# A graph layer on one core: one stage in TensorE's loop, single buffers, and paced gathers in the opening

## The chip, the core and the metric

The kernel runs on one core of a Trainium2 chip. The metric is the time of one launch on the device, in microseconds (us). The engines are named as the profile names them: PE is TensorE (PEld its weight loads), DVE is VectorE, ACT is ScalarE, POOL is GpSimd, SP is SyncE, which only issues DMAs here.

## What is computed

Inputs: 12,500 nodes with 16 channels (`x`), 400,000 edges with a source and a destination node (`src`, `dst`, sorted by `dst`), and two tables of edge attributes with 16 and 2 columns.

```python
dx = maximum(edge_attr_2[:, 0], 1e-6); inv_dx = 1 / dx
slope_e = edge_attr_2[:, 1] * inv_dx
diff = (x[dst] - x[src]) * inv_dx[:, None]
d1 = segment_sum(diff, dst) - segment_sum(diff, src)
S  = segment_sum(slope_e, dst)
u  = x - clip(dt, 0.01, 2.0) * (x * d1 + g * S)
x  = layernorm(x + u)
sums, counts = segment_sum(edge_attr_16, dst), segment_sum(ones, dst)
x  = layernorm(x + sums / where(counts > 0, counts, 1))
```

So each edge needs two rows of `x`, one by its destination and one by its source, and its payload is added at both ends.

## The kernel before

**Tiling.** The edges are cut into C = 125 chunks of 3,200; a chunk is 25 tiles (`J`) of 128 edges, one edge per partition. Since `dst` is sorted, the destinations of a chunk lie in a window of 112 nodes. The sources lie anywhere.

**The steps of a chunk**, in the order in which they depend on each other:

1. ACT `node_hot` (L506, L508) turns the chunk's destinations (`rel_all`, broadcast to all partitions by SP's `load_rel`) into the one-hot matrix `node_of_dst`.
2. PE `take_row` (L572), 25 narrow matmuls, takes x[dst] out of the window `xwin` (SP's `load_window`) into `ps_x`. The last of them raises `x_dst_ready`.
3. DVE piece `x_of_dst` (L792) reads it, `x_in` tells PE by `x_dst_added`; `diff` (L843) subtracts x[src], which 25 indirect gathers on POOL (L412) have brought; then `pay`, `lo`, `scale`, `scaled`, `left`, `parts` on DVE with casts on ACT between them (L480 or L489, L482, L484, L486).
4. DVE `dst_hot` (L924, five instructions) makes the one-hot matrix of the destinations, and PE `take_sum` (L583), 25 narrow matmuls, adds the chunk up into its window; DVE piece `window` (L893) adds that to `dst_sum`.
5. DVE `spread` (L882, ten instructions: five groups of five tiles, called fives here, in two halves k each) lays the payload out by the low three bits of the source.
6. The main work: for each tile DVE makes a one-hot row block of the source's high bits (`one_hot`, L947, 128x1568, one slot of the ring `hi_hot`), and PE multiplies it with the tile's two halves of `spread`: 2 x 4 matmuls of 128x392 (`tile`, L630 the first of four, L635 the other three), added up in `ps_src` over all 3,125 tiles.

**Staging.** Stage c does the main work of chunk c, steps 3 to 5 of chunk c+1 between the tiles of DVE (`PIECES` says after which tile), the sums of chunk c+1 on PE in its tiles 11 to 19, and the rows of chunk c+2 on PE in its tiles 0 to 12. PE's and DVE's loops hold two stages (`Fori(0, PAIRS)`), and `xwin`, `node_of_dst`, `dst_of_node` and `spread` have two buffers, by parity of the chunk.

**What sets the order.** Each engine runs its list in order, and semaphores join them. `hi_hot_free` starts at the credit `RING` (10) and is raised by PE with the last matmul of every tile; DVE asks for it at every fifth tile (`HOTS_FREE`), so at tile 5 of a chunk it needs all 25 tiles of the chunk before to be done. PE waits for `hi_hot_ready` every second tile. POOL's gathers come in groups of five, each waiting for `hi_hot_free` as well, but the 75 gathers of chunks 0, 1 and 2 wait for nothing but their indices. A chunk's spreads are announced once, by `chunk_ready`.

**The opening.** Before PE's loop stand `x_of_dst(0)`, `window_sums(0)` and `x_of_dst(1)`, each a run of 25 narrow matmuls. Tile 0 of stage 0 waits for the whole of chunk 0's spreads and, because the rows of chunk 2 begin with it, for `x_dst_added` of chunk 1 and `node_hot` of chunk 2.

## Time and profile before

| | |
|---|---|
| median of 3 runs | 5045.37 us (5037.35 to 5047.1) |
| the profiled execution | 5042.16 us |
| its span | 5040.3 us |
| PE busy | 4590.3 us, 91% of the span |
| DVE busy | 3983.5 us, 79% |
| POOL busy | 3415.4 us, 68% |
| ACT busy | 1446.6 us, 29% |
| granted clock of PE over the span | 0.975 |
| PE's first main matmul starts at | 112.81 us |

The profiled execution is 1.9 us longer than its span (5042.16 - 5040.3) and 3.2 us under the median. A row of a timeline gives the start, the busy time, the instructions that were joined, and in brackets how long the engine had stood idle and what ended it: `<-issue` is time in which it waited for nothing that the profile shows, `<-remote` is a semaphore whose raiser was done long before.

### The profile page before, as it was taken

What the parts mean: (1) busy time and instruction counts of PE and PEld (TensorE: products, weight loads), DVE (VectorE), ACT (ScalarE), POOL (GpSimd) and SP (SyncE); (2) the same over time, 40 slices, a digit from 0 to 9 for tenths busy, and PEclk for the clock granted to TensorE, in tenths of its full rate; (3) what the DMA queues carried; (4) which work ended last, traced back from release to release, by engine and by line L of the source; (5) the groups of instructions that cost most, each with busy time, mean ns of one, the idle gap of its engine ahead of it and who ended that gap; (6) DMA issues with size and microseconds to landing.
All of it is one profiled execution on the core that took longest, in us unless ns stands there. A gap on an engine that the chain in (4) does not pass through costs nothing. (4 is left out here: it accounts for less than half of the span.)

```text
span 5040.3 us, 72091 instructions
## 1 busy us (share of the span) xinstructions
PE 4590.3 (91%) x31379; PEld 1240.2 (25%) x12630; DVE 3983.5 (79%) x8600; ACT 1446.6 (29%) x1018; POOL 3415.4 (68%) x3133
## 2 busy tenths in 40 slices
PE   1999999999999999999999899999999999999997
PEld 0222222222222222222222222222222222222222
DVE  4887778778877787778887787778787788787887
ACT  3322232222322232222322233222322233222320
POOL 5667667767677677676677667767676776776760
PEclk8999999999999999999999999999999999999998
DMA  3111111111111111111111111111111111111110
GB/s 75 31 36 35 31 31 31 40 31 31 31 32 39 31 31 31 39 31 31 31 31 39 31 31 31 32 39 31 31 31 38 33 31 31 31 39 31 31 29 7
DMA packets 210295, 167.87 MB, mean 33 GB/s; under 512 B 124650, under 2 KB 193774, under 8 KB 210024
## 3 DMA queue, kind: packets, MB, share of 16 engines
q1 hardware_dynamic: 109798, 139.79, 8.7%
q0 software_dynamic: 100000, 25.80, 6.6%
q10 hardware_dynamic: 476, 2.01, 0.1%
q8 instruction: 11, 0.18, 0.0%
q14 instruction: 10, 0.08, 0.0%
HBM read 164.55 MB, written 2.81 MB: 33 GB/s over the span
## 5 line engine op out<-in xcount | busy, mean ns | idle before, releaser
L412 POOL DMA_INDIRECT x_src<-in_x_dram,src_i x3125 | 3410.5, 1091 | 1492.9 <-issue 871.0
L635 PE MATMUL ps_src<-hi_hot,spread_lo 128*128 128x392 bf16 x18750 | 4210.7, 332 | 77.7 <-issue 75.9
L947 DVE TENSOR_SCALAR hi_hot<-col_h,hi_f,scale 128x1568 bf16<-128x1568 f16 x3125 | 2238.7, 723 | 482.0 <-remote 270.3
L630 PE MATMUL ps_src<-hi_hot,spread_lo 128*128 128x392 bf16 x6250 | 2075.6, 332 | 210.0 <-issue 140.4
L630 PEld LDWEIGHTS ps_src<-hi_hot,spread_lo 128*128 128x128 f16 x6250 | 620.7, 99 | 1319.2 <-issue 952.8
L882 DVE TENSOR_TENSOR spread_lo<-spread_lo,halves 128x640 f16<-128x640 f16 x1250 | 616.8, 494 | 60.1 <-issue 59.9
L583 PEld LDWEIGHTS ps_w<-dst_of_node,parts 128*102 128x102 bf16 x3125 | 392.3, 126 | 1050.9 <-issue 1011.6
L572 PEld LDWEIGHTS ps_x<-xwin,node_of_dst 112*128 112x128 bf16 x3125 | 305.8, 99 | 1358.3 <-issue 1348.7
L572 PE MATMUL ps_x<-xwin,node_of_dst 112*128 112x48 bf16 x3125 | 584.5, 190 | 49.2 <-issue 41.7
L583 PE MATMUL ps_w<-dst_of_node,parts 128*102 128x112 bf16 x3125 | 501.3, 213 | 51.4 <-DVE parts L871 41.5
L482 ACT CAST parts<-pay 128x425 bf16<-128x425 f32 x125 | 72.4, 579 | 1616.0 <-DVE pay L846 1500.7
L496 ACT CAST parts<-a 128x400 bf16<-128x400 f32 x125 | 71.4, 571 | 1258.5 <-DVEq L909 765.0
L508 ACT ACTIVATE node_of_dst<-node_of_dst,ones 128x3200 bf16<-128x3200 bf16 x125 | 370.3, 2962 | 4.1
L506 ACT ACTIVATE node_of_dst<-rel_all,row_neg 128x3200 bf16<-128x3200 f16 x125 | 369.8, 2959 | 2.6 <-DMA rel_all<-rel_d 2.6
L489 ACT COPY spread_lo<-lo_hot 128x3200 f16<-128x3200 f16 x124 | 352.8, 2845 | 0.0
L792 DVE TENSOR_REDUCE x_dst<-ps_x 128x160 f32<-128x480 f32 x375 | 192.1, 568 | 193.4 <-issue 141.5
L924 DVE TENSOR_TENSOR dst_of_node<-col_h,dst_rel 128x560 bf16<-128x560 f16 x625 | 276.1, 443 | 1.0 <-issue 1.0
L484 ACT CAST halves<-scaled 128x400 f16<-128x400 f32 x125 | 65.6, 525 | 401.4 <-DVE scaled L860 310.7
L893 DVE TENSOR_TENSOR dst_sum<-dst_sum,ps_w 102x112 f32 x125 | 33.8, 271 | 163.6 <-remote 92.5
L940 DVE TENSOR_TENSOR left<-a,parts 128x400 f32<-128x400 f32 x125 | 72.1, 577 | 85.9 <-ACT parts L496 45.6
L486 ACT CAST parts<-left 128x425 bf16<-128x425 f32 x125 | 72.4, 579 | 87.3 <-issue 48.2
L498 ACT CAST parts<-left 128x400 bf16<-128x400 f32 x125 | 71.7, 574 | 80.4 <-DVE left L940 48.9
(114 smaller groups left out, 1200.5 us busy)
## 6 DMA issues: line engine op xcount, KB each, us to landing
rel_all<-rel_d SPq DMA_DIRECT2D x125, 800.0 KB
x_src<-in_x_dram,src_i POOLq DMA_INDIRECT x3125
a<-in_edge_attr_dram SPq DMA_DIRECT2D x125, 200.0 KB
a<-in_edge_attr_dram SPq DMA_DIRECT2D x125, 25.0 KB
src_i<-in_src_dram SPq DMA_DIRECT2D x125, 12.5 KB
dst_i<-in_dst_dram SPq DMA_DIRECT2D x125, 12.5 KB
xwin<-xparts_d SPq DMA_DIRECT2D x125, 10.5 KB
dst_sum<-in_dst_dram SPq DMA_DIRECT2D x1, 1400.0 KB
```

The costliest lines, as they stand in the source:

```text
L412: nc.gpsimd.indirect_dma_start(x_src[:, b, j * F:(j + 1) * F], None, x[:, :], bass.IndirectOffsetOnAxis(ap=src_i[:, b, j:j + 1], axis=0)). ...
L489: nc.scalar.copy(lo_rows[:, :, :, :], bc(lo_hot[:, :, :], 3, F)).then_inc(lo_rows_ready, 1)
L506: nc.scalar.activation(node_of_dst[:, b, :, :], rel_all[:, :, :], ACT.Abs, bias=row_neg[:, 0:1], scale=1.0).then_inc(node_diff_ready, 1)
L508: nc.scalar.activation(node_of_dst[:, b, :, :], node_of_dst[:, b, :, :], ACT.Relu, bias=ones[:, 0:1], scale=-1.0).then_inc(node_hot_ready, 1)
L572: return nc.tensor.matmul(ps_x[:, j // PER, (j % PER) * SPL * F:(j % PER + 1) * SPL * F], nodes[0:WIN, j, :], window, start=True, stop=True)
L583: return nc.tensor.matmul(ps_w[0:SPL * V, 0:WIN], parts[:, j, :, :].rearrange("p k v -> p (k v)"), hots[:, j, :], start=(j == 0), stop=(j ...
L630: return nc.tensor.matmul(out_bank, weights, moving, start=False, stop=stop)
L635: return nc.tensor.add_instruction(mybir.InstMatmult(name=nc.get_next_instruction_name(), engine=pe.engine, start_tensor_calc=False, stop_ ...
L792: yield v.tensor_reduce(out_t[:, q * PER:q * PER + n, :], ps_x[:, q, 0:n * SPL * F].rearrange("p (j k f) -> p j f k", k=SPL, f=F), AX, ALU ...
L882: ins = v.tensor_tensor(spread[:, b, five, q, :, :], lo_rows[:, five, :, :], bc(halves[:, five, q, :], 2, LO), ALU.mult)
L924: ins = v.tensor_tensor(dst_of_node[:, b, five, :].rearrange("p j (n t) -> p j n t", t=2), bc(col_h[:, 0:WIN].rearrange("p (n t) -> p n t" ...
L947: v.tensor_scalar(hi_hot[:, slot(b, j), :], col_h[:, :], hi_f[:, b, j:j + 1], scale[:, b, j:j + 1], ALU.is_equal, ALU.mult).then_inc(hi_ho ...
```

## The change

**PE's loop** holds one stage, run C-2 times. Its body reads the same addresses in every round: `xwin`, `node_of_dst`, `dst_of_node` and `spread` have one buffer each, the ring's slot is the tile's number modulo 13 and no longer depends on the chunk's parity, and the credit is `LEAD` = 12. DVE's, ACT's, SP's and POOL's loops still hold two stages.

**Spreads.** With one buffer, a five can be written only when PE has done the same five of the chunk before. `spread_half` waits for that and raises `spread_ready` per five; PE waits for it at tiles 0, 5, 10, 15 and 20. Six of a chunk's ten halves are made in the stage before, four (`late`) at tiles 2, 3, 8 and 8 of its own.

**The other single buffers.** `dst_hot` is made one chunk ahead, not two, at the same tiles of the stage; `dst_rel` and its copy `rel2` are two pieces. `node_hot(m)` waits for `x_dst_ready` of m (before m-1). SP loads the next window when `x_dst_ready` comes, and `rel_all` after `node_diff_ready`, no longer after `attr_left`.

**The opening.** Of chunk 1's gathers the first five are free, and its four other groups wait for `pay_ready`, `parts_ready` and the first `spread_ready` of chunk 0, and for its first tile; the groups of chunk 2 wait for every fourth tile. `x_of_dst(1)` stands ahead of `window_sums(0)` on PE; on ACT, `node_hot(1)` waits for `x_dst_ready` of chunk 0 and stands ahead of `finish(0)`, `node_hot(2)` ahead of `begin(1)`.

```diff
-    RING = 10
+    RING, LEAD = 13, 12
-        xwin = sb("xwin", [P, 2, SPL * F], bf16)
+        xwin = sb("xwin", [P, SPL * F], bf16)
...
-                  6: ["pay", "lo"], 7: ["scale"], 8: ["scaled"], 9: ["left"], 10: ["parts"],
-                  12: ["spread"], 13: ["spread"], 14: ["spread"], 15: ["spread"], 16: ["spread"], 17: ["spread"], 18: ["spread"],
-                  19: ["spread"], 20: ["spread"], 21: ["spread"], 22: ["slope"], 24: ["window", "attr_left"]}
+        EARLY = 3
+        LATE_AT = {2: 1, 3: 1, 8: 2}
+                  6: ["pay", "lo"], 7: ["scale"], 9: ["scaled"], 10: ["left"], 11: ["parts"], 12: ["dst_rel"],
+                  14: ["spread"], 15: ["spread"], 17: ["spread"], 18: ["spread"], 21: ["spread"], 22: ["spread", "slope"], 24: ["window", "attr_left"]}
...
-        def slot(c, j):
-            return (c % 2 * J + j) % RING
+        def slot(j):
+            return j % RING
...
-                sp.wait_ge(dst_hot_ready, m + 1)
+                sp.wait_ge(dst_rel_ready, m + 1)
                 load_dst(m + 2, b)
+                sp.wait_ge(x_dst_ready, m + 1)
+                load_window(m + 1)
+                sp.wait_ge(node_diff_ready, m + 2)
+                sp.sem_inc(rel_begun, 1)
+                load_rel(m + 2)
...
-            for g in range(3):
-                gather(g // 2, g % 2)
+            gather(0, 0)
+            gather(0, 1, first=[None, (pay_ready, 1), (parts_ready, 1), (spread_ready, 1), (hi_hot_free, LEAD + 1)])
+            gather(1, 0, first=[(hi_hot_free, LEAD + 4 * t) for t in range(1, 6)])
             with pool.Fori(0, (C - 3) // 2) as i:
-                gather(i + 1, 1, i * 2 * J + (RING + AHEAD))
-                gather(i + 2, 0, i * 2 * J + (RING + AHEAD + J))
+                gather(i + 1, 1, i * 2 * J + (LEAD + AHEAD))
+                gather(i + 2, 0, i * 2 * J + (LEAD + AHEAD + J))
...
                 act.wait_ge(scaled_ready, n + 1)
+                if not (isinstance(n, int) and n == 0):
+                    act.wait_ge(spread_ready, n * FIVES)
                 nc.scalar.copy(halves[:, :, 0, :], scaled[:, :, :]).then_inc(half0_ready, 1)
...
-                if not (isinstance(m, int) and m < 2):
-                    act.wait_ge(x_dst_ready, m - 1)
+                if not (isinstance(m, int) and m == 0):
+                    act.wait_ge(x_dst_ready, m)
...
-            node_hot(1, 1)
             act.wait_ge(tables_ready, 1)
             act.wait_ge(xparts_stored, 64)
+            act.wait_ge(rel_stored, 32)
+            node_hot(1, 1)
             finish(0)
+            node_hot(2, 0)
             begin(1, 0, 1)
-            node_hot(2, 0)
...
-                pe.wait_ge(chunk_ready, c + 1)
                 for j in range(J):
+                    if j % 5 == 0:
+                        pe.wait_ge(spread_ready, c * FIVES + (j // 5 + 1))
...
-            x_of_dst(0, 0, 0)
-            window_sums(0, 0, further_rows(0), first=True)
+            x_of_dst(0)
+            span = further_rows(0)
             pe.wait_ge(x_dst_added, 1)
-            x_of_dst(1, 0, 1)
-            with pe.Fori(0, PAIRS) as i:
-                for b in range(2):
-                    stage(i * 2 + b, b, i + 1, True, True)
-            stage(C - 3, 0, PAIRS + 1, True, True)
-            stage(C - 2, 1, 0, True, False)
-            stage(C - 1, 0, 0, False, False)
+            x_of_dst(1)
+            window_sums(0, span, first=True)
+            with pe.Fori(0, C - 2) as i:
+                stage(i, True, True)
+            stage(C - 2, True, False)
+            stage(C - 1, False, False)
...
-                        if not (isinstance(n, int) and n == 0):
-                            dve.wait_ge(hi_hot_free, (n - 1) * J + RING)
...
+            def spread_half(n, five, q):
+                if q == 0 and isinstance(n, int) and n == 0:
+                    dve.wait_ge(xparts_stored, 64)
+                elif q == 0:
+                    dve.wait_ge(hi_hot_free, n * J + (five * 5 + 5 + LEAD - J))
...
+                if q == HLV - 1:
+                    ins.then_inc(spread_ready, 1)
```

POOL's list in the opening, after the three iotas of its start (a row with `xN` stands for N such instructions). Before:

```order
L412 DMA x_src<-in_x_dram,src_i 128x16 [waits src_loaded0]
L412 DMA x_src<-in_x_dram,src_i 128x16 x24
L412 DMA x_src<-in_x_dram,src_i 128x16 [waits src_loaded1]
L412 DMA x_src<-in_x_dram,src_i 128x16 x24
L412 DMA x_src<-in_x_dram,src_i 128x16 [waits src_loaded0]
L412 DMA x_src<-in_x_dram,src_i 128x16 x24
```

POOL's list at the same place after the change, to the first group of chunk 2:

```order
L426 DMA x_src<-in_x_dram,src_i 128x16 [waits src_loaded0]
L426 DMA x_src<-in_x_dram,src_i 128x16 x24
L426 DMA x_src<-in_x_dram,src_i 128x16 [waits src_loaded1]
L426 DMA x_src<-in_x_dram,src_i 128x16 x4
L426 DMA x_src<-in_x_dram,src_i 128x16 [waits pay_ready]
L426 DMA x_src<-in_x_dram,src_i 128x16 x4
L426 DMA x_src<-in_x_dram,src_i 128x16 [waits parts_ready]
L426 DMA x_src<-in_x_dram,src_i 128x16 x4
L426 DMA x_src<-in_x_dram,src_i 128x16 [waits spread_ready]
L426 DMA x_src<-in_x_dram,src_i 128x16 x4
L426 DMA x_src<-in_x_dram,src_i 128x16 [waits hi_hot_free]
L426 DMA x_src<-in_x_dram,src_i 128x16 x4
```

Nothing has moved within POOL's list; after its thirtieth gather each further group of five has a step of chunk 0, and later a tile, to wait for.

DVE's list in a stage of its loop, tiles 1 to 4, before; `hi_hot` is the tile's one-hot block, `dst_of_node` is `dst_hot`:

```order
L947 TENSOR_SCALAR hi_hot<-col_h,hi_f,scale 128x1568
L924 TENSOR_TENSOR dst_of_node<-col_h,dst_rel 128x560
L947 TENSOR_SCALAR hi_hot<-col_h,hi_f,scale 128x1568
L924 TENSOR_TENSOR dst_of_node<-col_h,dst_rel 128x560
L947 TENSOR_SCALAR hi_hot<-col_h,hi_f,scale 128x1568
L924 TENSOR_TENSOR dst_of_node<-col_h,dst_rel 128x560
```

DVE's list from tile 2 to the wait ahead of tile 5 after the change; `dst_hots` is `dst_hot`, `spread_lo` a half of a five:

```order
L976 TENSOR_SCALAR hi_hot<-col_h,hi_f,scale 128x1568
L949 REGISTER_ALU
L951 TENSOR_TENSOR spread_lo<-spread_lo,halves 128x5x128 [waits hi_hot_free]
L905 TENSOR_TENSOR dst_hots<-col_h,dst_rel 128x560
L976 TENSOR_SCALAR hi_hot<-col_h,hi_f,scale 128x1568
L951 TENSOR_TENSOR spread_lo<-spread_lo,halves 128x5x128
L905 TENSOR_TENSOR dst_hots<-col_h,dst_rel 128x560
L976 TENSOR_SCALAR hi_hot<-col_h,hi_f,scale 128x1568
L905 TENSOR_TENSOR dst_hots<-col_h,dst_rel 128x560
L975 REGISTER_ALU
L976 TENSOR_SCALAR hi_hot<-col_h,hi_f,scale 128x1568 [waits hi_hot_free]
```

Two halves of a spread have come in ahead of tile 5 (two more stand after tile 8), from the stage's second part, where ten halves stood in ten successive tiles and six are left.

## Rows read from the trace of the kernel before

**Rows 1.** Windows: us, busy (x) of PE, PEld, DVE, ACT, POOL, clock, DMA share.

```profile
200.00:4880.00 4680.00, 4371.47 (x29869) 1173.29 (x11952) 3743.16 (x8122) 1365.84 (x957) 3269.55 (x2988) 0.98 0.15 33
```

**Rows 2.** Grouped by line, same stretch: busy us, mean ns | idle before.

```profile
L947 DVE TENSOR_SCALAR hi_hot<-col_h,hi_f,scale 128x1568 bf16<-128x1568 f16 x2989 | 2145.0, 724 | 477.3 <-remote 270.3 <-PE ps_src L635 192.7 <-issue 11.4
L882 DVE TENSOR_TENSOR spread_lo<-spread_lo,halves 128x640 f16<-128x640 f16 x1200 | 592.8, 494 | 57.6 <-issue 57.4
```

**Rows 3.** Waits view, same stretch: us in total, times, longest us.

```profile
DVE hi_hot L947 <- remote: 270.3, 97, 5.5
DVE hi_hot L947 <- PE ps_src L635: 192.7, 117, 4.7
...
PE ps_src L630 <- issue: 112.3, 156, 2.4
...
PE ps_src L635 <- issue: 74.0, 163, 1.8
PE ps_src L630 <- DVE hi_hot L947: 63.6, 99, 2.6
```

**Rows 4.** DMA view, same stretch: every queue with packets in it.

```profile
q1 hardware_dynamic: 102649, 130.06, 8.7%
q0 software_dynamic: 95583, 24.66, 6.8%
```

**Rows 5.** Timeline of PE where stage 24 begins, behind the loop's branch.

```profile
1046.37 0.33 PE L630 MATMUL ps_src<-hi_hot,spread_lo 128*128 128x392 bf16 x1
...
1047.03 0.33 PE L630 MATMUL ps_src<-hi_hot,spread_lo 128*128 128x392 bf16 x1
```

**Rows 6.** Timeline of POOL, PE and DVE early in stage 8.

```profile
424.30 0.94 POOL L412 DMA_INDIRECT x_src<-in_x_dram,src_i  x1 [0.30 <-issue]
...
426.05 0.33 PE L630 MATMUL ps_src<-hi_hot,spread_lo 128*128 128x392 bf16 x1 [1.33 <-issue]
...
426.89 0.69 DVE L947 TENSOR_SCALAR hi_hot<-col_h,hi_f,scale 128x1568 bf16<-128x1568 f16 x1 [4.01 <-remote]
```

**Rows 7.** Timeline of PE in the opening, 30 to 120 us.

```profile
39.60 1.16 PE L572 MATMUL ps_x<-xwin,node_of_dst 112*128 112x48 bf16 x25 [7.32 <-ACT node_of_dst L508]
82.31 2.54 PE L583 MATMUL ps_w<-dst_of_node,parts 128*102 128x112 bf16 x25 [41.55 <-DVE parts L871]
84.64 1.21 PE L572 MATMUL ps_x<-xwin,node_of_dst 112*128 112x48 bf16 x25
112.81 0.51 PE L630 MATMUL ps_src<-hi_hot,spread_lo 128*128 128x392 bf16 x1 [26.95 <-issue]
```

**Rows 8.** Timeline of DVE in the opening, same stretch.

```profile
74.22 1.54 DVE L792 TENSOR_REDUCE x_dst<-ps_x 128x160 f32<-128x480 f32 x3 [30.26 <-remote]
...
81.56 0.60 DVE L871 TENSOR_TENSOR parts<-left,parts 128x425 bf16<-128x425 f32 x1 [0.23 <-ACT parts L486]
...
85.19 0.26 DVE L893 TENSOR_TENSOR dst_sum<-dst_sum,ps_w 102x112 f32 x1
...
110.53 1.54 DVE L792 TENSOR_REDUCE x_dst<-ps_x 128x160 f32<-128x480 f32 x3 [21.68 <-remote]
...
117.66 0.57 DVE L843 TENSOR_TENSOR x_dst<-x_dst,x_src 128x400 f32<-128x400 f32 x1
```

**Rows 9.** Timeline of POOL: gathers 30, 50, 51 and 75, counted from 6.11.

```profile
44.35 0.94 POOL L412 DMA_INDIRECT x_src<-in_x_dram,src_i  x1 [0.30 <-issue]
...
69.31 0.94 POOL L412 DMA_INDIRECT x_src<-in_x_dram,src_i  x1 [0.30 <-issue]
80.59 1.06 POOL L412 DMA_INDIRECT x_src<-in_x_dram,src_i  x1 [10.34 <-DMA src_i<-in_src_dram]
...
111.19 0.94 POOL L412 DMA_INDIRECT x_src<-in_x_dram,src_i  x1 [0.30 <-issue]
```

**Rows 10.** Timeline of ACT in the opening.

```profile
44.01 2.96 ACT L508 ACTIVATE node_of_dst<-node_of_dst,ones 128x3200 bf16<-128x3200 bf16 x1
76.87 2.86 ACT L480 COPY spread_lo<-lo_hot 128x3200 f16<-128x3200 f16 x1 [29.90 <-DVE lo_hot L835]
```

More of the change, by code:

```diff
@@ L190, in gnn_kernel @@
         half0_ready = sem("half0_ready")
-        chunk_ready = sem("chunk_ready")
+        spread_ready = sem("spread_ready")
         win_sum_ready = sem("win_sum_ready")
@@ L411, in gather @@
                         pool.sem_inc(gather_begun, 1)
+                    if first is not None and j % GROUP == 0 and first[j // GROUP] is not None:
+                        pool.wait_ge(*first[j // GROUP])
+                        pool.sem_inc(gather_begun, 1)
                     nc.gpsimd.indirect_dma_start(
@@ L871, in finish @@
                     v.tensor_tensor(parts[:, :, 2, 0:F + 1], left[:, :, 0:F + 1], parts[:, :, 1, 0:F + 1], ALU.subtract).then_inc(parts_ready, 1)
+                if piece == "rel2":
+                    dve.wait_ge(dst_rel_ready, n + 1)
+                    step(v.tensor_copy(dst_rel2[:, :, :], bc(dst_rel[:, b, :], 2, 2)))
+                    done["rel2"] = count[0]
+                if piece == "dst_hot":
+                    at = done.setdefault(piece, 0)
+                    done[piece] += 1
+                    five = slice(at * 5, at * 5 + 5)
+                    if at == 0:
+                        settle_here("rel2")
+                        if not (isinstance(n, int) and n == 0):
+                            dve.wait_ge(win_sum_ready, n)
+                    ins = v.tensor_tensor(dst_of_node[:, five, :].rearrange("p j (n t) -> p j n t", t=2),
+                                          bc(col_h[:, 0:WIN].rearrange("p (n t) -> p n t", t=2), 1, 5),
+                                          bc(dst_rel2[:, five, :], 2, WIN // 2), ALU.is_equal)
+                    if at == FIVES - 1:
+                        ins.then_inc(dst_hot_ready, 1)
+                    else:
+                        step(ins)
                 if piece == "spread":
@@ L879, in finish @@
                         dve.wait_ge(lo_rows_ready, n + 1)
-                        if not (isinstance(n, int) and n == 0):
-                            dve.wait_ge(hi_hot_free, (n - 1) * J + RING)
-                    ins = v.tensor_tensor(spread[:, b, five, q, :, :], lo_rows[:, five, :, :], bc(halves[:, five, q, :], 2, LO), ALU.mult)
-                    if at == HLV * FIVES - 1:
-                        ins.then_inc(chunk_ready, 1)
-                    else:
-                        step(ins)
+                    spread_half(n, at // 2, at % 2)
                 if piece == "window":
@@ L946, in one_hot, with late @@
                     dve.wait_ge(hi_hot_free, c * J + j + min(HOTS_FREE, J - j))
-                v.tensor_scalar(hi_hot[:, slot(b, j), :], col_h[:, :], hi_f[:, b, j:j + 1], scale[:, b, j:j + 1],
+                v.tensor_scalar(hi_hot[:, slot(j), :], col_h[:, :], hi_f[:, b, j:j + 1], scale[:, b, j:j + 1],
                                 ALU.is_equal, ALU.mult).then_inc(hi_hot_ready, 1)
+            def late(c, j):
+                for _ in range(LATE_AT.get(j, 0)):
+                    at = done.setdefault("late", 0)
+                    done["late"] += 1
+                    spread_half(c, EARLY + at // 2, at % 2)
             def stage(c, b, k_next, k_later, tiles, does_finish, does_begin, pieces=PIECES):
```

125 lines of the change are left out of this document (57 added, 68 removed).

## The prediction, made blind

> **What bounds the kernel now.** I read the windows view first, to see which engine is full between the opening and the end. From 200 to 4880 us PE is busy for 4371.47 of 4680 us at a clock of 0.98, DVE for 3743.16, POOL for 3269.55 [rows 1]. 2,989 tiles ran there [rows 2], 119.6 chunks, so a chunk takes 4680 / 119.6 = 39.1 us. The reader should see an engine that is nearly full, in a kernel where DVE with 31.3 us a chunk (3743.16 / 119.6) has only 7.8 us of slack.
>
> How short could a chunk be? Half a tile on PE takes 1047.03 - 1046.37 = 0.66 us [rows 5]. Fifty are 33.0 us, and the 50 narrow matmuls come on top; PE's whole busy time, in which slow stretches count in full, is 4371.47 / 119.6 = 36.6 us a chunk [rows 1]. So between 2.5 us (39.1 - 36.6) and 6 us of a chunk, 300 to 740 us in all, are stalls and half clock. The waits view says which. Main matmuls waited 112.3 + 74.0 us with cause "issue", 63.6 us for DVE's `hi_hot`; DVE waited 270.3 us for a semaphore whose raiser was done long before ("remote") and 192.7 us for PE [rows 3].
>
> Stage 8 shows what these have in common: POOL's last gather of a run of them ends at 425.24 (424.30 + 0.94); PE, which had stood, goes on at 426.05, and DVE, idle for 4.01 us, sees PE's finished tiles at 426.89 [rows 6]. The opening shows it at full size. PE's rows of chunk 0 are done at 39.60 + 1.16 = 40.76 [rows 7], and DVE sees it at 74.22 [rows 8], 4.0 us after POOL's fiftieth gather ends at 70.25 [rows 9]. The rows of chunk 1 are done at 84.64 + 1.21 = 85.85 and seen at 110.53, when POOL is at its last gathers (111.19). PE's first main matmul comes at 112.81. I read this as: while POOL issues gathers back to back, what PE announces comes through late, and is let through when POOL pauses. One row speaks against it: the window's sums, done at 84.85, are seen at once, at 85.19 [rows 7 to 9], while POOL gathers too.
>
> **The opening, step by step.** The change makes POOL pause after gather 30, which ends at 44.35 + 0.94 = 45.3 [rows 9]; before, it ran on to gather 50.
> - `x_dst_ready` of chunk 0 is then seen 1.7 us (stage 8) to 4.0 us (the opening) after the pause: 47.0 to 49.3; I take 48.
> - From there `parts` took 81.56 + 0.60 - 74.22 = 7.9 us [rows 8]. Now `node_hot(1)` stands ahead of `finish(0)` on ACT: two instructions of 2.96 us from 48 to 54. The copy that was second in the chain began 76.87 - 74.22 = 2.65 us after the rows were seen [rows 10]; it now begins 6.0 us after: 3.3 us more. `parts` come at 48 + 7.9 + 3.3 = 59.2.
> - `pay_ready` (about 51) has let a group of five gathers go, which ends by 57.5: five at 1.25 us ((69.31 - 44.35) / 20). `parts_ready` lets the next go at 59.2, and `spread_ready`, 1 us later (two halves at 0.494 [rows 2]), the third: POOL is then busy for 12.5 us, to 71.7.
> - PE's rows of chunk 1 need `node_hot(1)` (54) and end at about 56. If their update comes through only at the long pause, ACT and DVE see it at 71.7 + 1 = 72.7. Then ACT's `node_hot(2)`, which PE's tile 0 waits for and which now waits for this update, takes 5.9 us: the first main matmul at about 78.6, where it was at 112.81. Gain 34 us.
> - If the update slips through in the 1.7 us between 57.5 and 59.2, ACT starts `node_hot(2)` right after `finish(0)`, at about 59, and the first main matmul comes at 65.5: gain 47 us. If gathers only lengthen the waits partly, less; 15 us is my lower bound with the mechanism right, 0 with it wrong.
> - The pacing has a price. Chunk 1's last five gathers wait for tile 0. PE starts at 1.2 GHz (a first matmul of 0.51 us, against 0.33 at full clock [rows 5, 7]); I take 2.7 us for it, twice 2 x 0.66. The five are issued 6.3 us later and land perhaps 2 us after that, 11 us after the start. DVE wants them for `diff` 117.66 - 112.81 = 4.9 us after the start [rows 7, 8], behind tile 5. PE has six blocks (6 x 1.33, and 1.3 more for the slow tile), which last to 9.3 us; DVE then needs 0.57 for `diff` and 0.72 for the next block, to 12.3. So PE loses 3 us, between 0 and 6.
>
> Opening in all: -34 + 3 = -31 us, between -47 and 0.
>
> **The steady stages, part by part.**
> - Removed: nothing. The same 50 wide halves, 50 narrow matmuls, 25 `hi_hot`, 10 spread halves and 5 `dst_hot` run in a chunk; `dst_rel2` is now a copy of `dst_rel`, a small instruction for a small one.
> - Four spread halves, 4 x 0.494 = 1.98 us [rows 2], go from the stage's second part into DVE's first nine tiles, where `dst_hot`, `diff`, `pay`, `lo` and `scale` stand already. `scaled`, `left`, `parts` come a tile later there, for the same room. DVE's slack of 7.8 us a chunk covers it if its lead over PE is over 2 us at the stage's start. If the lead is gone, PE pays up to 1.98 us a chunk, 244 us over 123 stages; if it never is, 0. I take 0, with the next item.
> - The credit is 12. At tile 5 DVE needed all 25 tiles of the chunk before; now it needs 23. Where DVE stands there, it is let go up to two tiles of PE earlier, about 2.7 us. It waited 214 times (97 + 117) for 463 us in all [rows 3]. What of that reaches PE is 63.6 us plus part of the rest; gains between 0 and 65 us. I set this against the late halves: even, +-25 us. That is a choice: both act at the same place, one later by 1 us (two halves ahead of tile 5), the other earlier by 2.7 us in the stages where it bites.
> - PE's waits: five `spread_ready` instead of one `chunk_ready`. Waits that are met cost nothing visible: PE's cadence in rows 5 includes one each two tiles. The wait at tile 15 needs halves of DVE's tiles 2 and 3, that at tile 20 those of tile 8: twelve tiles and more of cover. On DVE, a five's write waits for the chunk before at the same five: at tile 2, PE's tile 20 of the chunk before, so five to seven tiles of lead are allowed, as the ring allows anyway. Nothing.
> - ACT's `node_hot` for two chunks ahead now waits for PE's tile 12 of the stage, and has to be done by its tile 25: 5.9 us in about 17. Covered; ACT is busy for 29% of the span.
> - SP: the window and the 800 KB of `rel_all` are asked for earlier, past the load of 200 KB. DMA share is 0.15 [rows 1]. Nothing.
> - PE's loop branches at every stage, not every second. Stage 24 begins behind a branch and the cadence holds at 0.66 us [rows 5]: nothing.
> - The end (separate memory for the final sums) keeps its steps: nothing, +-2 us.
>
> **The sum.** 5042.16 - 31 + 0 = 5011.2 for an execution like the profiled one. That one is 3.2 us under the median of the runs shown, so I forecast a median of 5014.
>
> A rule that would give another time is that a smaller loop body takes less instruction loading. Between 200 and 4880 us only the two queues of data have packets [rows 4], and none that loads instructions. The Trainium skill's page "Runtime: NRT & Kernel Launch", section "Instruction fetch mechanics", says that a taken branch whose target lies outside the two blocks held forces a fetch before the engine goes on; by that, PE's loop, cut in half, would stand less. By the rule rival F below would hold; by rows 4 and 5, nothing changes there.
>
> **Rivals.**
> - *G, the lead pays.* The looser credit outweighs the late halves: PE no longer waits 63.6 us for `hi_hot` [rows 3], which is its price, and the first half after each such wait no longer runs at half clock. For it: 117 waits of DVE for PE. Against: 270.3 of DVE's 463 us are "remote", which a credit only helps where PE's announcements have come through. Time 5014 - 64 = 4950.
> - *F, the shorter body removes the "issue" stalls.* Then 112.3 + 74.0 = 186.3 us go as well [rows 3]: 5014 - 186 = 4828. For it: they are called "issue" and PE's program shrinks. Against: rows 4 and 5, and that in stage 8 PE resumes with POOL's pause [rows 6].
> - *N, the opening's stalls aren't POOL's.* Then what holds PE's update until 74.22 and 110.53 stays, and the change adds as much as it takes: 5045. For it: the update of 84.85 that was seen at once.
> - *S, slower.* DVE's first part becomes the bound: its two halves ahead of tile 5 and two behind tile 8 arrive on a lead that is gone. Stage 8 is such a place: PE stood until DVE's tile [rows 6], and it happens in some of the 99 waits of PE for DVE [rows 3]. At 1.0 us a chunk, about half of 1.98, the price is 123 us: 5014 + 123 = 5137. It decides as soon as it passes 31 / 123 = 0.25 us a chunk. Against: the credit.
>
> **How the numbers follow.** Forecast 0.42 (own range 4985 to 5035), G 0.17, F 0.06, N 0.10, S 0.25. A measurement of this kernel can tell about 0.2%, 10 us, from no change. Faster by more (under 5035): forecast, G and F, 0.65, and a little of S at its small end: 0.66. Within: N, 0.10. Slower (over 5055): S, 0.24. The range leaves out F and the larger half of S, 2 in 10: 4915 to 5090.
>
> **What the profile after would show.** Step right: DVE sees the first rows at 47 to 49, PE's first main matmul comes at 65 to 80, POOL's gaps stand after gathers 30 and 35. Steady: 39.1 us a chunk from 200 us on, PE's waits for `hi_hot` near 64 us. G: that wait under 20 us and the chunk under 38.6 us. F: PE's "issue" under 50 us. S: PE's wait for `hi_hot` over 150 us and its places at tiles 4 to 12. N: the first main matmul after 100 us. What would make it wrong above all is a new stall in each of 123 stages, since 0.3 us there outweighs the whole opening.

## The result, and the profile after

The changed kernel takes 4976.94 us (median of 4 runs, 4964.91 to 4982.2) against 5046.24 for the kernel before beside it: a ratio of 0.986, 95% interval 0.9835 to 0.9886, or 69 us less. The forecast was 5014, 31 us less. The profiled execution took 4982.2 us with a span of 4980.4, 59.9 us under that of before. Where these 59.9 us lie is the first thing to read.

PE's timeline in the opening, 30 to 180 us, answers to [rows 7]:

```profile
39.32 1.16 PE L592 MATMUL ps_x<-xwin,nodes_mem 112*128 112x48 bf16 x25 [6.91 <-ACT nodes_mem L527]
53.16 1.16 PE L592 MATMUL ps_x<-xwin,nodes_mem 112*128 112x48 bf16 x25 [12.69 <-ACT nodes_mem L527]
58.34 2.54 PE L603 MATMUL ps_w<-dst_hots,parts 128*102 128x112 bf16 x25 [4.02 <-DVE parts L892]
68.56 0.51 PE L650 MATMUL ps_src<-hi_hot,spread_lo 128*128 128x392 bf16 x1 [7.67 <-DVE hi_hot L976]
...
83.18 0.34 PE L650 MATMUL ps_src<-hi_hot,spread_lo 128*128 128x392 bf16 x1 [3.86 <-DVE hi_hot L976]
...
121.04 0.45 PE L650 MATMUL ps_src<-hi_hot,spread_lo 128*128 128x392 bf16 x1 [2.62 <-issue]
122.46 0.49 PE L655 MATMUL ps_src<-hi_hot,spread_lo 128*128 128x392 bf16 x1 [0.98 <-issue]
123.87 0.48 PE L655 MATMUL ps_src<-hi_hot,spread_lo 128*128 128x392 bf16 x1 [0.92 <-issue]
...
176.48 0.34 PE L650 MATMUL ps_src<-hi_hot,spread_lo 128*128 128x392 bf16 x1 [2.62 <-issue]
```

DVE's, same stretch, beside [rows 8]:

```profile
46.98 1.54 DVE L812 TENSOR_REDUCE x_dst<-ps_x 128x160 f32<-128x480 f32 x3 [4.05 <-remote]
...
66.29 1.54 DVE L812 TENSOR_REDUCE x_dst<-ps_x 128x160 f32<-128x480 f32 x3 [1.28 <-issue]
...
80.20 0.57 DVE L864 TENSOR_TENSOR x_dst<-x_dst,x_src 128x400 f32<-128x400 f32 x1 [5.94 <-DMA x_src<-in_x_dram,src_i]
...
139.33 0.69 DVE L976 TENSOR_SCALAR hi_hot<-col_h,hi_f,scale 128x1568 bf16<-128x1568 f16 x1 [14.72 <-remote]
```

The first main matmul comes at 68.56, 44.25 us earlier than at 112.81. But 176.48 is the first matmul of stage 2, and in the kernel before that stood at 190.27:

```profile
190.27 0.33 PE L630 MATMUL ps_src<-hi_hot,spread_lo 128*128 128x392 bf16 x1
```

So 13.8 us are left there, and 30.5 us were given back inside stages 0 and 1: they take 46.2 and 61.7 us, where they took 37.1 and 40.4 (stage 1 began at 149.92 in the kernel before and at 114.75 now). The reader can see how: at 83.18 PE had waited 3.86 us for a block that DVE made late, since `diff` stood for chunk 1's gathers until 80.20; then, from 121 to 139 us, PE issued its main matmuls at best one every 1.4 us and DVE stood for 14.72 us, while POOL gathered from 81.44 to 134.50 with no pause at all. The other 46 us (59.9 - 13.8) came bit by bit in the steady stages. Windows view, 200 to 4820 us (columns as in [rows 1]), DVE's rows by line, and the waits, to hold against [rows 1 to 3]:

```profile
200.00:4820.00 4620.00, 4317.16 (x29794) 1170.32 (x11919) 3626.80 (x8099) 1370.52 (x953) 3241.84 (x2980) 0.98 0.14 33
```

```profile
L976 DVE TENSOR_SCALAR hi_hot<-col_h,hi_f,scale 128x1568 bf16<-128x1568 f16 x2978 | 2041.3, 702 | 109.1 <-remote 68.4 <-PE ps_src L655 36.9 <-issue 1.1
...
L925 DVE TENSOR_TENSOR dst_sum<-dst_sum,ps_w 102x112 f32 x119 | 32.4, 272 | 517.3 <-remote 299.5 <-PE ps_w L603 118.1 <-issue 99.6
```

```profile
PE ps_src L650 <- issue: 89.5, 105, 3.9
PE ps_src L650 <- DVE hi_hot L976: 77.4, 91, 3.9
...
PE ps_src L655 <- issue: 38.6, 81, 1.1
...
PE ps_src L650 <- DVEq L860: 36.5, 16, 5.7
```

and, of the kernel before (200 to 4880 us), the wait that answers to the last of them:

```profile
PE ps_src L630 <- DVEq L839: 3.9, 2, 2.2
```

A chunk takes 4620 / (2978 / 25) = 38.8 us, where it took 39.1. DVE's idle time has moved: ahead of `hi_hot` it fell from 477.3 to 109.1 us, and ahead of the window sum at tile 24 it grew to 517.3. DVE now mostly runs through tile 5 and stands at the stage's end. PE's waits for issue on main matmuls went from 186.3 to 128.1 us; those for `hi_hot` did not fall (63.6, now 77.4). And DVE's new place to stand has a price: the wait at L860 (L839 before) is PE's tile 0 waiting for `x_dst_added`, which DVE raises soon behind that stop, and it grew from 3.9 to 36.5 us. So PE's idle time is nearly what it was, 2.58 us a chunk before ((4680 - 4371.47) / 119.6) and 2.54 now ((4620 - 4317.16) / 119.1). The 0.36 us that a chunk got shorter lies almost wholly in PE's busy time, 36.6 us a chunk before and 36.2 now, though one main matmul takes as long as before (332 ns on average). Matmuls that follow each other closely overlap in this view and matmuls that come one by one do not, so fewer slow stretches of issue would show in this way; how much of the 0.36 us that is was not worked out.

### The profile page after: what moved, and what is told of

The parts are those of the page before. It is cut to its first block and busy times, and to the rows that moved or that the text cites. A ratio compares the mean times of both kernels' runs of the same rounds, so it can differ in the third digit from the quotient of the medians.

```text
span 4980.4 us, 73841 instructions
## 1 busy us (share of the span) xinstructions
PE 4553.8 (91%) x31379; PEld 1241.0 (25%) x12630; DVE 3877.3 (78%) x8600; ACT 1460.2 (29%) x1018; POOL 3400.9 (68%) x3133
## 5 line engine op out<-in xcount | busy, mean ns | idle before, releaser
L976 DVE TENSOR_SCALAR hi_hot<-col_h,hi_f,scale 128x1568 bf16<-128x1568 f16 x3125 | 2140.3, 701 | 126.0 <-remote 85.1
L603 PEld LDWEIGHTS ps_w<-dst_hots,parts 128*102 128x102 bf16 x3125 | 392.7, 127 | 1014.1 <-issue 974.6
L592 PE MATMUL ps_x<-xwin,nodes_mem 112*128 112x48 bf16 x3125 | 585.0, 190 | 61.6 <-issue 41.9
L592 PEld LDWEIGHTS ps_x<-xwin,nodes_mem 112*128 112x128 bf16 x3125 | 306.7, 99 | 1326.6 <-issue 1317.0
L603 PE MATMUL ps_w<-dst_hots,parts 128*102 128x112 bf16 x3125 | 501.1, 214 | 14.9 <-issue 10.8
L525 ACT ACTIVATE nodes_mem<-rel_all,row_neg 128x3200 bf16<-128x3200 f16 x125 | 370.6, 2965 | 372.2 <-PE ps_x L592 234.9
L527 ACT ACTIVATE nodes_mem<-nodes_mem,ones 128x3200 bf16<-128x3200 bf16 x125 | 370.6, 2965 | 4.1
L905 DVE TENSOR_TENSOR dst_hots<-col_h,dst_rel 128x560 bf16<-128x560 f16 x625 | 276.5, 443 | 34.2 <-issue 19.2
L848 DVE TENSOR_TENSOR parts<-left,parts 128x400 bf16<-128x400 f32 x125 | 72.8, 582 | 35.5 <-issue 35.5
L517 ACT CAST parts<-left 128x400 bf16<-128x400 f32 x125 | 71.8, 575 | 80.6 <-DVE left L969 57.4
```

Of the source, the lines that this page charges most:

```text
L525: nc.scalar.activation(node_of_dst[:, :, :], rel_all[:, :, :], ACT.Abs, bias=row_neg[:, 0:1], scale=1.0).then_inc(node_diff_ready, 1)
L527: nc.scalar.activation(node_of_dst[:, :, :], node_of_dst[:, :, :], ACT.Relu, bias=ones[:, 0:1], scale=-1.0).then_inc(node_hot_ready, 1)
L592: return nc.tensor.matmul(ps_x[:, j // PER, (j % PER) * SPL * F:(j % PER + 1) * SPL * F], nodes[0:WIN, j, :], window, start=True, stop=True)
L603: return nc.tensor.matmul(ps_w[0:SPL * V, 0:WIN], parts[:, j, :, :].rearrange("p k v -> p (k v)"), hots[:, j, :], start=(j == 0), stop=(j ...
L905: ins = v.tensor_tensor(dst_of_node[:, five, :].rearrange("p j (n t) -> p j n t", t=2), bc(col_h[:, 0:WIN].rearrange("p (n t) -> p n t", t ...
L976: v.tensor_scalar(hi_hot[:, slot(j), :], col_h[:, :], hi_f[:, b, j:j + 1], scale[:, b, j:j + 1], ALU.is_equal, ALU.mult).then_inc(hi_hot_r ...
```

## The experiments

Each group of runs had the kernel before run beside it on the same chip, and each group had a chip of its own (for the first comparison, the chip isn't recorded). The median of the kernel before differed widely between groups, and that turned out to be the main finding, so it stands with each: group 1 5031.7 us, group 2 5043.0, group 3 4959.6, group 4 4499.6, group 5 4956.0. Every experiment below is given as its ratio to the kernel before of its own group. Two ratios are compared closely only within a group. Between groups 1 and 2 and the first comparison (5046.2), where the kernel before took nearly the same, they are compared as well, but groups 1 and 2 are two different chips and that of the first comparison is unknown, so a difference of a few tenths of a per cent between them shows nothing. The changed kernel exactly as it is ran only in the first comparison and in group 4.

### Group 1 (before at 5031.7): the opening, the pacing, the credit

**b_open**, the kernel before with the paced opening.

```diff
-            for g in range(3):
-                gather(g // 2, g % 2)
+            gather(0, 0)
+            gather(0, 1, first=[None, (pay_ready, 1), (parts_ready, 1), (parts_ready, 1), (hi_hot_free, RING + 1)])
+            gather(1, 0, first=[(hi_hot_free, RING + 4 * t) for t in range(1, 6)])
```

> The kernel before with the paced opening alone: chunk 1's gather groups wait for pay_ready, parts_ready, parts_ready and tile 0, those of chunk 2 for every fourth tile. Theory P (POOL's back-to-back gathers hold up what PE announces and issues): PE's first main matmul at 65 to 85 us, not 112.8, and 14 to 40 us less in all, 5006 to 5032. Rival (the order on PE and ACT brought the earlier start, not the pauses): still over 105 us, and 5046.

Ratio 0.9982 (0.9969 to 0.9995): 9 us less. PE's first main matmul came at 76.05 us, without the new order of PE and ACT, so the pauses bring the earlier start. And what is left of it is small: the same slow stretch follows, here from about 131 to 152 us.

**a_free**, the changed kernel with the opening's gathers ungated.

```diff
-            gather(0, 1, first=[None, (pay_ready, 1), (parts_ready, 1), (spread_ready, 1), (hi_hot_free, LEAD + 1)])
-            gather(1, 0, first=[(hi_hot_free, LEAD + 4 * t) for t in range(1, 6)])
+            gather(0, 1)
+            gather(1, 0)
```

> The changed kernel with the 75 gathers of chunks 0 to 2 ungated, as before. Theory P: the first main matmul comes after 100 us again and the time rises by the net worth of the paced opening, 14 us (what the start of stage 2 showed) to 44 us: 4991 to 5021. Rival (order on PE and ACT): 4977.

Ratio 0.9858 (0.9834 to 0.9883), beside 0.986 for the changed kernel in the first comparison, and 0.9861 for a_each below on the same one. The first main matmul is at 121.29 us, as Theory P had it, but the time is the rival's: in the whole time no worth of the pacing can be seen. At the start of stage 2 it can: that comes at 194.02 us here and at 172.64 in a_each. The steady stages then take it back, with 38.5 us a chunk here (4620 / (3001 / 25)) and 38.7 in a_each; why isn't known. The trace of this run shows best what a nonstop run of gathers does to PE. PE's 25 narrow matmuls of the window sum, which took 2.54 us in [rows 7]:

```profile
67.47 1.14 PE L603 MATMUL ps_w<-dst_hots,parts 128*102 128x112 bf16 x10 [3.88 <-issue]
69.40 0.25 PE L603 MATMUL ps_w<-dst_hots,parts 128*102 128x112 bf16 x1 [0.80 <-issue]
71.50 0.25 PE L603 MATMUL ps_w<-dst_hots,parts 128*102 128x112 bf16 x1 [1.85 <-issue]
74.29 0.25 PE L603 MATMUL ps_w<-dst_hots,parts 128*102 128x112 bf16 x1 [2.53 <-issue]
```

Ten go at once, and then one every 2.1 to 3.5 us. PE waits for no semaphore; its instructions come slowly. So it is not only PE's announcements that are held up.

**a_each**, each steady gather with a wait of its own (`if pace is not None:` in place of `... and j % GROUP == 0:`).

> The changed kernel with each steady gather waiting for a tile of its own (group of 1 in place of 5), the same lead. Theory P: POOL pauses after nearly every gather, so PE's waits with cause issue (178 us in the steady stretch after) fall under 90 us and the time is 50 to 200 us less, 4780 to 4930. Rival (the stalls are not of POOL's making, or only its total matters): within 10 us of 4977. Second rival: more waits on POOL make gathers late, over 4990.

Ratio 0.9861 (0.9836 to 0.9885): no gain. But the edit did not produce what it was meant to: in its trace POOL has 254 pauses of over 0.65 us between its 3,125 gathers, against 229 in the changed kernel's, since a POOL that is behind runs through its waits. It leaves open what pauses would do.

**a_credit10**, `RING, LEAD = 13, 10`.

> The changed kernel with the credit set back from 12 to 10, ring still of 13 slots. Theory C (the steady gain of 0.39 us a chunk, 46 us, comes from the looser credit): 5023, and DVE waits for PE at tile 5 again, over 300 us in all. Rival (it comes from the one-stage loop on PE, or from the spreads' new places): within 10 us of 4977.

Ratio 0.9832 (0.981 to 0.9854), or 4946 us. The looser credit is not the cause of the steady gain. DVE's waits ahead of `hi_hot` grew to 239.9 us, under the 300 that Theory C had asked for.

### Group 2 (before at 5043.0): the loop, the spreads, the gathers' start and their price

**a_pe2**, two stages in PE's loop again.

```diff
-            with pe.Fori(0, C - 2) as i:
-                stage(i, True, True)
+            with pe.Fori(0, PAIRS) as i:
+                for b in range(2):
+                    stage(i * 2 + b, True, True)
+            stage(C - 3, True, True)
```

> The changed kernel with two stages in TensorE's loop again (61 rounds, and one stage more behind it), all else as changed; ratio to the kernel before is 0.986 for the changed one. Theory L (the steady gain comes from the shorter loop body): ratio 0.995 or more. Theory D (it comes from DVE's spreads: four of ten halves out of the stage's second part, into its first): within 0.003 of 0.986.

Ratio 0.9824 (0.9807 to 0.984), a little under Theory D's range. Theory L falls: with the loop's two stages back the whole gain is there.

**b_late**, the kernel before, double buffers and all, with the new places of the spread halves.

```diff
-                  6: ["pay", "lo"], 7: ["scale"], 8: ["scaled"], 9: ["left"], 10: ["parts"],
-                  12: ["spread"], 13: ["spread"], 14: ["spread"], 15: ["spread"], 16: ["spread"], 17: ["spread"], 18: ["spread"],
-                  19: ["spread"], 20: ["spread"], 21: ["spread"], 22: ["slope"], 24: ["window", "attr_left"]}
+                  6: ["pay", "lo"], 7: ["scale"], 9: ["scaled"], 10: ["left"], 11: ["parts"],
+                  14: ["spread"], 15: ["spread"], 17: ["spread"], 18: ["spread"], 21: ["spread"], 22: ["spread", "slope"], 24: ["window", "attr_left"]}
+        LATE_AT = {2: 1, 3: 1, 8: 2}
...
-                pe.wait_ge(chunk_ready, c + 1)
+                    if j % 5 == 0:
+                        pe.wait_ge(spread_ready, c * FIVES + (j // 5 + 1))
```

> The kernel before (two buffers, ring and credit of 10, two-stage loops, ungated opening) with the changed kernel's places of the spread halves alone: fives first, six halves at tiles 14 to 22, four at tiles 2, 3, 8, 8 of the own stage, five waits for spread_ready on TensorE, scaled, left and parts at tiles 9 to 11. Theory D: DVE's wait for hi_hot (463 us in the steady part) falls under 200 us, that of its window sum grows, and the ratio is 0.984 to 0.992. Rival (these places cost, theory S of the prediction; the gain is from single buffers' other moves): 1.000 or more.

Ratio 0.9849 (0.9832 to 0.9866): most of the gain, with an ungated opening, credit 10 and two buffers. It is 74 us less than the kernel before, where a_pe2, which has all but the short loop, is 89 us less. Stage 2 begins at 189.1 us, so nearly all of it is steady. A chunk takes 4620 / (2997 / 25) = 38.5 us. DVE's rows show the move of the stall, here by halves:

```profile
DVE dst_sum L891 <- remote: 277.5, 52, 5.8
...
DVE hi_hot L959 <- PE ps_src L638: 170.2, 113, 5.0
...
DVE hi_hot L959 <- remote: 86.5, 48, 2.8
```

DVE's idle time ahead of `hi_hot`, 272.7 us in all, did not fall under the 200 that Theory D had forecast. And here too PE's waits changed in kind: those for issue on main matmuls are 65.3 us, those for `hi_hot` 116.3 and those for `x_dst_added` 58.7.

**a_ahead16**, steady gathers let go after 16 tiles of PE in place of 10 (`AHEAD, GROUP = 16, 5`).

> The changed kernel with the steady gathers let go six tiles later (16 tiles done in place of 10), so that in the opening chunk 3's gathers don't queue up behind chunk 2's. Theory P: the stretch of back-to-back gathers at 81 to 135 us breaks up, stage 1 takes under 50 us instead of 60.6, and the time falls by 10 to 20 us: ratio 0.982 to 0.984. Rival (POOL's total decides, or gathers come late for DVE in the steady stages): 0.986 or more.

Ratio 0.9782 (0.9768 to 0.9796), the fastest in its group that has all its gathers, and better than either theory had it. Beside a_pe2 of the same group it is 19 us less. About half of that is the opening's: stage 2 begins at 168.25 us, where it begins at 178.18 in a_pe2. But stage 1 still takes 55.4 us, not under 50. A chunk takes 4620 / (3006 / 25) = 38.4 us, where it takes 38.5 in a_pe2; over 119 chunks that is the other half.

**a_fifth**, the changed kernel with one gather in five.

```diff
+                    if j % 5:
+                        continue
...
-                    dve.wait_ge(gathered[b], (k + 1) * 16 * J)
+                    dve.wait_ge(gathered[b], (k + 1) * 16 * FIVES)
```

> The changed kernel with 5 of a chunk's 25 gathers (tile 0 of each five), whose rows stand in for the other four: the x[src] of four fifths of the edges is left out. It prices the gathers. Theory P: PE's waits with cause issue go under 40 us, DVE's remote waits go, half clock goes, and a chunk takes 35.1 to 35.6 us: 4430 to 4520 us in all. Rival (the stalls have another cause): chunk over 37.5 us, 4750 or more.

4494.55 us, ratio 0.8909 (0.8897 to 0.8922). Windows, waits and DVE's row of this run:

```profile
200.00:4420.00 4220.00, 4219.02 (x30049) 1168.78 (x12000) 3557.31 (x8168) 1366.81 (x955) 728.32 (x593) 1.00 0.11 32
```

```profile
PE ps_src L652 <- DVE hi_hot L979: 1.0, 1, 1.0
```

```profile
L979 DVE TENSOR_SCALAR hi_hot<-col_h,hi_f,scale 128x1568 bf16<-128x1568 f16 x3007 | 1999.8, 681 | 2.9 <-PE ps_src L657 0.2
```

PE is busy for 4219 of 4220 us at full clock, a chunk takes 4220 / (3007 / 25) = 35.1 us, and its only wait of note is 1.0 us. So all of the stalls, 3.7 us a chunk beside the changed kernel's 38.8 and 3.4 beside a_pe2's 38.5 on the same chip, go with four fifths of the gathers. The edit takes away POOL's work and the transfers that it starts, so it doesn't tell which of the two holds PE up.

### Group 3 (before at 4959.6)

**b_mid**, the kernel before with the fives first and five waits, its ten halves left at tiles 12 to 21.

```diff
-                    q, five = divmod(at, FIVES)
+                    five, q = divmod(at, HLV)
```

> The kernel before, its ten spread halves where they stood (tiles 12 to 21 of the stage before), but fives first and with TensorE's five waits for spread_ready: the order without the move. Theory D (what counts is that four halves leave DVE's second part): ratio 0.998 to 1.002. Rival (the finer announcement lets TensorE begin a chunk on less): 0.985 to 0.990, as with the four late halves (0.9849).

Ratio 1.0036 (1.002 to 1.0051), just over Theory D's range. Its trace holds a warning: DVE stands at the stage's end here too, with 149.7 us ahead of `hi_hot` and 358.0 us ahead of the window sum (361.3 in b_late), and without a gain.

```profile
DVE hi_hot L946 <- PE ps_src L635: 103.8, 62, 4.5
...
DVE dst_sum L892 <- remote: 334.2, 85, 6.9
```

**b_ahead16**, the kernel before with `AHEAD` of 16.

> The kernel before with the steady gathers let go after 16 tiles in place of 10. In the changed kernel this was worth 0.8%. If that came from the opening's queue of gathers alone, which this kernel doesn't have (all 75 are done when TensorE's tiles begin): 1.000. If the later start helps every steady stage, as the changed kernel's chunk of 38.4 us against 38.8 says: 0.990 to 0.994.

Ratio 1.0087 (1.0069 to 1.0106), slower than either range: the later start of the gathers does not help every kernel on every chip.

**a_combo**, the changed kernel with `AHEAD` 16, credit 10 and two stages in PE's loop.

> The changed kernel with the three settings that did no harm or good one by one: gathers after 16 tiles, credit of 10, two stages in TensorE's loop. If their gains over the changed kernel add up (0.8% + 0.3% + 0.4%): ratio 0.971. If they act on the same stalls: 0.976 to 0.979.

Ratio 0.9999 (0.9986 to 1.0012). All three of its settings had looked harmless or good; here the variant is level with the kernel before, which itself takes 1.7% less than in group 2. That is where I saw that the gain is not the same everywhere. Without the changed kernel or b_late in this group, b_mid says only that the order alone brought no gain here. Whether b_late's gain in group 2 needs the four late halves, or would have come with the order and the five waits alone, isn't shown.

**a_gap**, `AHEAD` 16 and a memset behind every fifth steady gather.

```diff
+                    if pace is not None and j % GROUP == GROUP - 1:
+                        pool.wait_ge(idle_done, gaps + (j // GROUP + 1))
+                        pool.sem_inc(gather_begun, 1)
+                        nc.gpsimd.memset(idle[:, :], 0.0).then_inc(idle_done, 1)
```

> The changed kernel with gathers after 16 tiles (ratio 0.978) and, behind every fifth steady gather, a 128x384 memset on POOL, some 0.4 us in which it makes no gather. Theory P1 (a short pause in a run of gathers is enough to let TensorE's announcements and issue through): stalls shrink, 0.960 to 0.974. Theory P2 (what counts is how long POOL needs for its gathers, or the engine has to be wholly idle): 0.978 or more.

Ratio 0.9898 (0.9877 to 0.9918): 1.0% under a_combo, and the fastest here. That fits with a pause of 0.5 us behind every five gathers helping PE where gathers hold it up. It isn't shown, since a_combo differs from it in the credit and in PE's loop as well, and the changed kernel with `AHEAD` 16 alone did not run in this group. The ratio itself lies in Theory P2's range, which was set by the ratio of another chip.

### Group 4 (before at 4499.6): the same kernels without stalls

**a_same**, the changed kernel as it is.

> The changed kernel as it is, beside the kernel before and the three below on one chip. In the last group of runs the kernel before took 4959.6 us, not 5031 to 5046, and a variant of the changed kernel that I expected at 0.971 to 0.979 came out level with it. If the stalls of the kernel before depend on the chip (or its state that day) and the change removes only what they add: ratio 0.995 to 1.000 where before is near 4960, 0.984 to 0.988 where it is near 5040. Rival (the three settings combined cost 1.4% together): 0.984 to 0.988 in either case.

Ratio 1.0047 (1.0034 to 1.0061): the change costs 21 us here. Both of my ranges were wrong, as was the idea that two cases were all there were. The kernel before takes 4499.6 us, next to the 4495 of one gather in five. The trace of a_same has all of its gathers, POOL as busy as ever, and no stall; windows, waits:

```profile
200.00:4420.00 4220.00, 4215.28 (x29956) 1165.47 (x11965) 3644.46 (x8156) 1370.46 (x957) 3295.59 (x2988) 1.00 0.18 36
```

```profile
DVE dst_sum L925 <- PE ps_w L603: 302.4, 120, 3.2
...
PE ps_src L650 <- DVE hi_hot L976: 0.2, 1, 0.2
```

**b_late2**, b_late once more.

> The kernel before with the new places of the spread halves alone (as b_late, ratio 0.985 there). Theory D (these places are the whole gain): the same ratio as the changed kernel's of this group, within 0.004, whichever that is. Rival (single buffers and credit carry part): over 0.004 above it.

Ratio 1.0035 (1.0021 to 1.0048). Within 0.004 of a_same again, as Theory D had it: the spreads' places carry the change's loss as well, 16 of 21 us. Its opening has ungated gathers, and PE and DVE are not held up in it:

```profile
52.47 2.54 PE L586 MATMUL ps_w<-dst_of_node,parts 128*102 128x112 bf16 x25 [11.88 <-DVE parts L875]
54.81 1.12 PE L575 MATMUL ps_x<-xwin,node_of_dst 112*128 112x48 bf16 x25
```

```profile
58.62 1.54 DVE L796 TENSOR_REDUCE x_dst<-ps_x 128x160 f32<-128x480 f32 x3 [1.13 <-issue]
```

The same 25 sums that dripped out over tens of microseconds in a_free take 2.54 us, with POOL gathering at its pace of 1.25 us. So a nonstop run of gathers is not enough by itself.

Where the 16 us lie: in every second stage PE comes to its tile 8 late, mostly by 0.2 to 0.3 us, 17 us in all in a_same and 16 in b_late2. PE asks for blocks 8 and 9 together, and DVE makes two spread halves between them. The rest of a_same's loss is about its opening: stage 2 begins at 143.79 us, and at 139.68 in b_late2. PEld, a_same, stage 4:

```profile
225.62 0.10 PEld L650 LDWEIGHTS ps_src<-hi_hot,spread_lo 128*128 128x128 f16 x1 [0.31 <-DVE hi_hot L976]
```

**a_gap2**, a_gap once more.

> The changed kernel with gathers after 16 tiles and a 128x384 memset (0.508 us each) on POOL behind every fifth steady gather; 0.9898 of before in the last group, where before was at 4960. Theory P1 (pauses in POOL's runs let TensorE's announcements through): 0.8% to 1.5% under the changed kernel of this group. Rival (only the later start of the gathers counts): 0.6% to 0.9% under it, as with that alone.

Ratio 1.05 (1.0486 to 1.0515), far over both ranges. With no stall to relieve, the pause and the later start of the gathers are pure cost: POOL has 25 x 1.25 + 5 x 0.5 = 34 us of work in a chunk of 35, the gathers land late, and DVE and PE wait:

```profile
PE ps_src L657 <- DVE hi_hot L983: 190.2, 206, 1.3
DVE x_dst L871 <- DMA x_src<-in_x_dram,src_i: 165.9, 102, 2.4
```

**b_fifth**, the kernel before with one gather in five (edit as in a_fifth).

> The kernel before with 5 of a chunk's 25 gathers (tile 0 of each five), whose rows stand in for the other four: the x[src] of four fifths of the edges is left out. Theory P with D: without the long runs of gathers a chunk takes 35.1 us in this kernel too, so the places of the spreads are worth nothing by themselves: 4490 to 4520 us. Rival (DVE's second part bounds the kernel before also without stalls): chunk of 36 us or more, over 4600.

4495.34 us, ratio 0.9991 (0.9982 to 1.0). It says little about its group's question, since the kernel before is at 4499.6 with all gathers. But it equals a_fifth of group 2 (4494.55): with a fifth of the gathers the kernel takes the same time where the stalls are and where they aren't. What differs between groups 2 and 4 is what the other four fifths of the gathers cost the kernel before, 548 us (5043.0 - 4494.6) against 4.

### Group 5 (before at 4956.0)

**a_apart** and **a_apart16**, the changed kernel with `LATE_AT = {2: 1, 3: 1, 7: 1, 9: 1}` and an ungated opening, the second with `AHEAD` 16 too.

> The changed kernel with its two spread halves of tile 8 set apart, at tiles 7 and 9, and with the opening's gathers ungated. On the chip without stalls (before at 4500) the changed kernel was 21 us slower: TensorE's tile 8 took 1.51 us instead of 1.38 on average (16 us in 120 stages), and the paced gathers cost 4 to 6. Theory S8 (the pair of halves between blocks 8 and 9 makes TensorE wait): there 1.000 to 1.001. On a chip with stalls (before at 5030 to 5046): 0.982 to 0.987, as the ungated changed kernel (0.9858).

> The same with the steady gathers let go after 16 tiles. On a chip without stalls DVE then waits for x[src] at tile 5 (theory: gathers land up to 2 us late): 1.001 to 1.01. On a chip with stalls: 0.975 to 0.980, as the changed kernel with this setting (0.9782).

Ratios 1.0096 (1.0078 to 1.0114) and 1.0151 (1.0131 to 1.0171). This was a group of the middle kind, for which I had written no number. Neither is a better version there, and whether 7 and 9 mend tile 8 where nothing stalls wasn't seen.

## Why the prediction was wrong, point by point

The direction and the range (4915 to 5090) held; the size did not: 69 us for 31. Two terms of the sum were wrong, in opposite directions.

- **What holds PE: right as far as it went.** The prediction read the late announcements as the work of back-to-back gathers. a_fifth shows that the stalls go with the gathers (3.7 us of every chunk), and a_free that PE's own issue is slowed as well. What it missed is that this is not a fixed property of the kernel: in group 4 the same gathers cost 4 us in all.
- **"`x_dst_ready` of chunk 0 ... I take 48": right**, 46.98. `parts` came at 58.2, forecast 59.2.
- **The second update: the other branch.** I took the long pause (main matmuls at 78.6) over the 1.7 us gap (65.5). The second update was through when ACT began `node_hot(2)` at 57.4. That was before the gap too: POOL's gather of 56.49 ran to 57.70, so this update, like the window's sums in the kernel before, came through while POOL gathered. PE began at 68.56.
- **"So PE loses 3 us, between 0 and 6": the failed step of the opening.** Measured were 30.5 us. The wait behind tile 5 was priced right (3.86 us of PE). Not seen at all was that pacing only moves the gathers: 32 of the 75 that had run ahead of PE's work now run beside it, with those of chunk 3 right behind, and late in the unbroken run from 81 to 135 us PE was slowed to one matmul per 1.4 us. Net -13.8 us by the trace for -31 forecast; the paced opening alone is worth 9 us in b_open, and nothing that can be measured in a_free.
- **"I take 0" for the steady stages: the term that was mis-sized most**, 0 +-25 for a measured -46 us in the profiled execution. I had weighed the late halves only as a load on DVE's first part, against the credit. b_late, which has the spreads' new order and places alone, has 74 of the 89 us of its group's a_pe2, so the gain is in this part, and a_credit10 shows that it needs no looser credit. The mechanism stays open. The traces show that DVE's stop moved from tile 5 to tile 24 and that PE's waits for issue shrank, but the stop alone explains nothing: in b_mid it moved as well, without a gain, and behind it PE now waits 36.5 us for `x_dst_added`. That four halves have left DVE's second part, so that it is further ahead by tile 24, is my reading and isn't shown.
- **Rival G** had a time (4950) that lies a little nearer to 4977 than mine, for a wrong reason: a_credit10 keeps the gain with the old credit, and PE's wait for `hi_hot` rose. Its half clock behind "each" such wait was too much as well: of the 99 waits in the kernel before, 14 have matmuls of 0.5 us right behind them.
- **Rival F**: a_pe2 rules it out. Rows 4 and 5 were right on that.
- **Rival N**: false; b_open starts PE at 76.
- **Rival S**: false in the measured case and real where nothing stalls: 0.13 us a chunk at tile 8, below its point of decision of 0.25, but there is no opening gain to set against it there, and the change loses 0.47%.

What stays open is why a chip, or its state, makes gathers hold up PE. The runs show three levels of the kernel before, 5031 to 5046, 4956 to 4960 and 4500 us, with no difference in the kernel, and no row of the profile names the cause. Since no chip ran in two groups, a property of the chip and its state at the time can't be told apart. Also open is the changed kernel's own ratio at the middle level: only variants of it ran there, at 0.9898 to 1.0151.

## What to carry to other kernels

When an engine's wait ends "remote" or by "issue" on an engine that waited for nothing, price it by taking the suspect's work away (here four fifths of the gathers) before counting any single cure: what a cure for stalls is worth has to be measured on each chip. Here the same change ranged from 1.4% gained to 0.5% lost, and its worth did not simply follow the size of the stalls: at the middle level, with some 460 us of them (4956 - 4495), two variants close to it lost 1.0 and 1.5%. Work that is moved out of an opening's way has to be followed to where it lands. And when an engine's stop moves to another place in the stage, look at what stands behind the new place: here it was the announcement that the other engine's next stage begins with.

## What was not expected of the hardware

- The same kernel took 4499.6, 4956 to 4960 and 5031 to 5046 us in different groups, each with a chip of its own. In the fastest, PE was busy for 4215 of 4220 us at full clock in the changed kernel (a_same), with 25 gathers of 1.1 us each per chunk beside it.
- Under stalls PE's instructions themselves come slowly: main matmuls 1.40 us apart in the changed kernel, narrow ones 2.1 to 3.5 us apart in a_free, with cause issue, and a run of ten narrow ones passes there before it sets in.
- A 128x384 memset on POOL takes 0.508 us. Behind every fifth gather, with the gathers let go later, it was part of the fastest variant in group 3 and of one that took 5.0% more than the kernel before in group 4.
